# Tile stage of a six-layer attention kernel: four pieces issued at other places

## What is computed

```python
for i in range(DEPTH):                       # 6 layers
    x = attn_layer(shift_tokens(x), ...) + x
    x = ffn_layer(shift_tokens(x), ...) + x
# attn_layer: q, k, v = x @ Wqkv   (16 heads of 64)
#   q = l2norm(q) * qs; k = l2norm(k) * ksc; rotate both by tables (cos, sin, scale)
#   windows of 32 tokens see their own and the previous window:
#   sim = q k^T * 8, masked; attn = softmax(sim); out = attn v; out @ Wo
# ffn_layer: xn = layernorm(x); a, gate = split(xn @ W1 + b1)
#   a * gelu(gate) @ W2 + b2
```

## Time and profile before

| | us |
|---|---|
| runs | 2463.4 (median), 2463.25, 2467.93 |
| profiled execution | 2469.18 |
| its span (first to last instruction) | 2467.4 |
| busy in the span: PE | 2082.4 (84%) |
| DVE | 1832.7 (74%) |
| ACT | 1507.3 (61%) |
| POOL | 1163.3 (47%) |

### The profile page before, as it was taken

The page is one execution under the profiler, slowest core; times in us unless marked ns, Lnnn a source line. Parts: engine busy times, 40 slices in busy tenths (PEclk is TensorE's granted clock), DMA queues, the critical chain, the costliest instruction groups (busy, mean ns, idle before and its releaser), DMA issues.

```text
span 2467.4 us, 87755 instructions
## 1 busy us (share of the span) xinstructions
PE 2082.4 (84%) x34492; PEld 1484.1 (60%) x34492; DVE 1832.7 (74%) x3797; ACT 1507.3 (61%) x2993; POOL 1163.3 (47%) x1373
## 2 busy tenths in 40 slices
PE   6888899876688888888888898888888888888886
PEld 4556654454466666666566665666666666666663
DVE  6777855576687787777777877787687777777873
ACT  4666733364566676666766666666666666766663
POOL 1111100001666666555665556666566655665660
PEclk9999999997899999999999999999999999999998
DMA  4000000001121232222222212222222222222221
GB/s 101 2 2 1 2 1 0 1 1 43 51 69 52 51 87 70 60 65 56 78 62 69 59 52 78 68 71 52 63 77 66 62 67 63 77 60 58 64 57 30
DMA packets 94732, 126.36 MB, mean 51 GB/s; under 512 B 27485, under 2 KB 42467, under 8 KB 94307
## 3 DMA queue, kind: packets, MB, share of 16 engines
q1 hardware_dynamic: 94306, 120.54, 18.7%
HBM read 21.91 MB, written 1.05 MB: 9 GB/s over the span
## 4 chain that ended last, share of the span: by engine, by line
PE 43%; DVE 17%; issue 11%; ACT 9%; POOL 1%; ACTq 0%; DVEq 0%; DMA 0%; POOLq 0%; SPq 0%
PE pj L567 10%; PE sc L567 10%; PE oo L567 10%; PE tr L570 8%; ACT arena L1782 7%; PE tr L567 5%; DVE arena L1608 3%; DVE arena L1614 3%; DVE arena L1606 2%; DVE xn L1225 1%; DVE arena L1628 1%; DVE arena L1630 1%; PE oo L570 1%; DVE stats L1212 1%; ACT sc L1782 0%
## 5 line engine op out<-in xcount | busy, mean ns | idle before, releaser
L2172 POOL TENSOR_TENSOR arena<-arena 128x1024 f32<-128x1024 f32 x192 | 456.7, 2379 | 260.2 <-DVE arena L1608 249.1
L1782 ACT ACTIVATE arena<-tr 128x512 f32<-128x512 f32 (+2 forms) x874 | 456.5, 571 | 136.2 <-PE tr L570 86.4
L1782 ACT ACTIVATE arena<-pj 128x512 f32<-128x512 f32 x576 | 333.9, 592 | 264.0 <-PE pj L567 259.7
L570 PE MATMUL tr<-ident,arena 128*128 128x128 f32 x2974 | 435.2, 282 | 67.1 <-ACT arena L1782 53.3
L1782 ACT ACTIVATE arena<-arena 128x16 f32<-128x16 f32 (+6 forms) x808 | 354.9, 453 | 212.3 <-DVE arena L1623 113.6
L1606 DVE TENSOR_TENSOR arena<-pj,rtab 128x512 f32<-128x512 f32 x384 | 262.9, 685 | 275.2 <-ACT arena L1782 174.9
L570 PEld LDWEIGHTS tr<-ident,arena 128*128 128x128 f32 x2974 | 345.6, 143 | 152.8 <-issue 59.1
L2188 POOL TENSOR_TENSOR arena<-arena 128x1024 f32<-128x1024 f32 x192 | 370.4, 1929 | 17.9 <-POOL arena L2184 1.2
L567 PE MATMUL oo<-slab,arena 64*32 64x64 f32 (+1 forms) x12416 | 234.0, 230 | 59.4 <-issue 24.7
L1608 DVE TENSOR_TENSOR arena<-pj,rtab 128x512 f32<-128x512 f32 x384 | 261.5, 681 | 0.0
L1614 DVE TENSOR_REDUCE arena<-arena 128x8 f32<-128x512 f32 x384 | 259.6, 676 | 0.0
(11 more groups left out here) (275 smaller groups left out, 3824.3 us busy)
## 6 DMA issues: line engine op xcount, KB each, us to landing
slab<-arena SPq DMA_DIRECT2D x576, 128.0 KB
slab<-arena SPq DMA_DIRECT2D x336, 64.0 KB
wqkv<-in_L_ffn_Wqkv SPq DMA_DIRECT2D x18, 512.0 KB, 3.5
wo<-in_L_ffn_Wo SPq DMA_DIRECT2D x6, 512.0 KB, 4.2
w<-in_L_ffn_W SPq DMA_DIRECT2D x6, 341.0 KB
YT<-in_L_attn_x SPq DMA_DIRECT2D x4, 256.0 KB, 3.7
arena<-in_L_ffn_W SPq DMA_DIRECT2D x1, 1024.0 KB
out_x<-arena SPq DMA_DIRECT2D x4, 256.0 KB, 2.2
```

The lines of the kernel that those rows point to most:

```text
L570: return nc.tensor.transpose(o, i, ident[0:i.shape[0], 0:i.shape[0]])
L1782: return nc.scalar.activation(o, i, f, **k)
L2172: p_.tensor_tensor(r_, r_, rb[:, k, :], ALU.add).then_inc(sum_ok, 1)
```

## The change

Four pieces are issued at other places in `slot`. No operation is added or taken away.

1. PE, t = 0: `ff_up(m2, 2)` now stands before `window_scores(g - 1, .., 1)` instead of behind it.
2. DVE: `tables(l + 1)` stands at the start of b = 2, t = 0 instead of the end of b = 1, t = 2.
3. ACT: the exponential of tile g-1 is no longer the last step of slot g; it stands in slot g+1 (there as tile g-2) between `square(g, 0)` and `square(g, 1)`.
4. ACT, t = 3: the output copies `out_` stand before `ln_finish` instead of behind it.

The order of steps inside each moved piece is kept, and its semaphores count one tile further back, since it now runs one slot later.

```diff
@@ PE
                 if t != 0 and d_:
                     out_()
-                if c_:
-                    window_scores(g - 1, (t - 1) % T, 1)
                 if t == 0 and m2 is not None:
                     pe.wait_ge(on_ok, g - 1 if d_ else NTILE)
                     ff_up(m2, 2)
+                if c_:
+                    window_scores(g - 1, (t - 1) % T, 1)
                 if t == 0 and d_:
                     out_()
@@ DVE
+                if new and b == 2 and t == 0:
+                    tables(l + 1)
                 if new:
...
-                if new and b == 1 and t == 2:
-                    tables(l + 1)
@@ ACT
                 def exp_():
-                    ac.wait_ge(t_sub, g)
-                    wait(ac, e_tr, g * 2 - 2)
-                    wait(ac, sm_ok, g - 1)
+                    ac.wait_ge(t_sub, g - 1)
+                    wait(ac, e_tr, g * 2 - 4)
+                    wait(ac, sm_ok, g - 2)
...
                 if new:
                     wait(ac, ss_ok, g * 4 - 1)
                     square(g, 0)
+                if d_:
+                    exp_()
+                if new:
                     wait(ac, ss_ok, g * 4)
                     square(g, 1)
...
+                if d_:
+                    out_()
                 if t == 3 and m1 is not None:
                     ac.wait_ge(lc_ok, m1 + 1)
                     ln_finish(LNB, LNB_BANKS[1], m1, lcur[:, 0:1], lcur[:, 1:2], hB)
-                if d_:
-                    out_()
                 if new:
                     inverse_root(g, 1)
                     copy_v(g, t, 1)
-                if c_:
-                    exp_()
```

## The result

| | before | after |
|---|---|---|
| median of the runs, us | 2465.66 (four runs) | 2376.65 (four runs) |
| fastest and slowest, us | 2463.25, 2469.19 | 2372.35, 2377.54 |
| profiled execution, us | 2469.18 | 2377.54 |
| its span, us | 2467.4 | 2375.7 |
| granted clock over the whole | 0.974 | 0.976 |

The ratio of the times is 0.9634, with a 95% interval of 0.9616 to 0.9653: the changed kernel is faster by 89.0 us in the medians and by 91.7 us in the span of the two profiled executions. The prediction was 2390.8 us with a range of 2374 to 2424, from a gain of 72.6 us. Direction, mechanism and range held; the gain was some 16 us larger than forecast, and so lies outside the 60 to 77 us that had the largest chance (0.40), in the class of rival (a) and a little more (0.24).

What follows compares the result with a forecast made beforehand. PE was taken to set the pace, losing time in short waits mostly ended by ACT. Terms of 42.7 + 4.5 - 1.2 + 27.6 + 7 = 80.6 us, less 8 for late instructions, gave 72.6: median 2390.8 us, range 2374 to 2424.

Steps and rivals of the forecast that it cites:

- rival (a): Nothing is lost to late PE instructions: 80.6 us less, median 2382.8; chance 0.24, with gains up to 95 us.
- What bounds the kernel: PE sets the pace and loses time in short waits; ACT ends the longest, 134.8 us between 700 and 2400 us.
- The up-product and the exponential: t = 0 to t = 1: PE's waits shrink by 2.1 us per sequence, 1.4 at b = 3; 42.7 us.
- The exponential at the other slots: Gains 4.5 us from t = 2 to t = 3, loses 1.2 at t = 0 of b = 0, otherwise 0.
- The norm's end: t = 3: PE's wait for the output copies before the output product goes, except part at b = 3; 27.6 us.
- The tables: Moved to b = 2, they hide in DVE's idle time and shorten PE's norm wait at b = 1; 7 us.
- What may eat of it: PE instructions that arrive late take back 8 us, a quarter of 33 us of waits without a releaser.
- The gross of 80.6: Sum of the forecast's terms in us before the deduction for late instructions: 42.7 + 4.5 - 1.2 + 27.6 + 7.
- (b): PE's transposes release DVE at t = 1, so the first term is 1.2 per sequence: gain 53 us, median 2410; chance 0.11.
- (c): Late PE instructions take half of the gross: gain 40 us, median 2423; chance 0.11.
- (d): No change: ACT and DVE give back what each piece gains, as when later soft1 holds ACT; chance 0.04.
- (e): Slower: ACT held longer at the exponential, PE waits 2.8 us at t = 1, clock drops; +19 us, median 2482; chance 0.06.

Runs made afterwards that it cites:

- the first experiment: The changed kernel with the exponential put back at the end of its slot, the other three pieces still moved: 2400.4 us, ratio 0.9724.
- norm first: The changed kernel with DVE's `ln_apply` at t = 3 put before the sums of the squares: 2372.5 us, ratio 0.9603.
- copy first: The changed kernel with ACT's last value copy of t = 0 put before its inverse root: 2379.2 us, ratio 0.9628.

## Why the prediction was right, and where it was off

**What bounds the kernel: right.** PE set the pace, ACT's ends of a few chains set PE's waits, and taking those waits away gave the time: the four rows fell by 68.8 us and the time by 89. A removed wait gave some 0.16 us more than its listed length (below), and pauses without a releaser went with them.

**The up-product and the exponential: mechanism right, size a little low.** The signs it named came out as follows: 0.77 instead of 0.5 before the second projection; 1.89 instead of 2.4 us of DVE idling before soft1; no wait before the down-product. Predicted were 2.1 us per plain sequence, 1.2 from the up-product and 0.9 from the exponential. The table of starts shows 0.39 + 0.95 + 0.94 = 2.28 in the sequence that the prediction had read, but 1.9 in a plain one, 0.95 and 0.94. Two readings were off. The half of the scores was priced at 1.2 us from 1669.55 to 1670.73, a stretch that holds the pause of 0.16; where no pause stands, the third up-product starts 1.11 us behind the last value projection before and 0.23 now, so the chain on ACT begins 0.88 us earlier and not 1.2. And b = 3 gained the same 1.9 as the others, where 1.4 was forecast. Over the 22 sequences it is 3.8 + 21.0 + 20.6 = 45.4 us against 42.7, and 3.8 of the 45.4 are pauses that went. The runs give 52 to 54 us for the two parts against 46.0 with the other slots; most of what is above lies in the pause of the draining pipeline and in the filling (below). The order of the two pieces itself cost and saved nothing, as predicted. Whether the pauses went because the instructions stand at other positions or for another reason, no run here tells apart.

**The exponential at the other slots: the size about right, by another path.** At t = 3 of the sequence that was traced, the probabilities' transposes come 0.61 us earlier, counted from the down-product. PE's wait for ACT before them fell from 1.50 to 1.01 us; it stood in the trace and the prediction didn't name it, though it is part of the 44.2 us of the earlier trace rows. But the norm then has PE wait 0.44 us longer (0.58 to 1.02). The prediction let the norm's wait shrink by 0.25; it grew, since PE got there sooner than DVE. Over the stage it is 18.0 to 20.5 us, +2.5, where -4.5 was forecast. From the down-product to the output product the exponential's move is worth 3.7 us over the 22 sequences when it is undone and 2.3 when it is done alone, against 4.5 - 1.2 = 3.3; two executions of the changed kernel differ by 2.7 us there, so this is no proof.

**The norm's end: right** (27.6 forecast, 28 measured by undoing it), by two errors that cancel. At b = 3 waits of 5.3 us in sum stayed, up to 1.47, instead of 5 times 0.67, since the split of the next key weights and its load stand in front, which I had named and not priced. In the other sequences a removed wait gave more than its listed length: 1.46 for 1.30, 1.75 for 1.58.

**The tables: not told.** 7 forecast, 3 to 4 by the runs, 3 to 8 by the starts, and by the runs alone not told from nothing. The mechanism is seen: b = 1 is 1.8 to 2.0 us a pass shorter. At b = 2 the tables do stand in an idle stretch: they end at 1604.73, and DVE still waits 0.35 us for ACT's square before it rotates (1605.08).

**What may eat of it: wrong, by the whole 8 us.** The step that failed took the pauses named "issue" to grow when waits ahead of them go. Their sum fell, 47.9 to 40.0, and another of 2.40 us, behind 2400 us, went too. Rival (a) was right. A reading was off as well: the four edges make 2.68 + 2.65 + 2.82 + 2.40 = 10.6 us of the sum, not about 15, so 37 us were left for the other places and not 33. The Trainium skill (Runtime: NRT & Kernel Launch, Instruction fetch mechanics) holds that fetching in straight code is hidden and that only a taken branch breaks it. Its result for the sum was right. Its reason isn't what the traces show: pauses of 0.88 and 0.95 us stand in straight code, and these two moved by 16 products when 16 were put in front.

**How the sum closes.** The gross of 80.6 was made of 5.5 passes, 14.7 a pass. The four middle passes gained 14.7 each. Of the 91.7 us of the span, 11 lie beyond 80.6, and most of them lie where the pipeline fills and drains, which the prediction didn't count: 3.1 us before the first output product, 3.1 after the last one, and 3.8 instead of 1.8 in the second sequence, which has no feed-forward part behind it. In the filling, ACT's exponential stood on the way of every tile; there PE's waits before transposes, some of the first in the stage, fell from 2.22 and 1.92 us to 1.73 and 1.42. The runs bear this out: the first output product starts at 681.8 to 682.2 us in the three traces with the exponential in its old place and at 677.3 to 679.8 in the eleven with it moved. In the draining it is the up-product and the pause of 2.40 us.

So for the medians: 80.6, less no supply, plus some 8 from the two ends, is 89. That it closes so well is partly luck, as the terms above are off in both directions by 3 to 8 us.

**The rivals.** (b) falls by the first experiment. (c) and (d) fall by the time. For (e), slower through a low clock, the largest wait of PE for ACT outside the edge is now 1.5 us. The granted clock was 0.50 (1.2 instead of 2.4 GHz) for at least 4 us behind three of the four edges of the changed kernel. The windows (us; busy us of PE, PE's weight load, DVE, ACT, POOL; granted clock; DMA share; GB/s) behind the third edge and around the first:

```profile
1732.00:1736.00 4.00, 3.47 (x71) 2.51 (x72) 3.82 (x10) 0.00 (x0) 0.92 (x1) 0.50 0.59 168
1150.00:1166.00 16.00, 9.47 (x170) 6.62 (x168) 11.74 (x28) 8.09 (x16) 7.75 (x12) 1.00 0.42 112
```

The prediction let one wait of about 2.7 us decide. These rows don't bear that out. The waits at the four edges were 2.54, 2.61, 2.48 and 2.82 us; behind the first the clock stayed at 1.00, and behind the others it fell only 5 to 6 us later, where the kernel before had it low right behind its 2.82.

## What to carry to other kernels

When one engine sets the pace and loses its time in short waits, list the waits by what ended them, find the few places in the code where they stand, and move what stands ahead of the late step on the *other* engine, first of all work whose reader is far off. Price it from start to start, not by the listed waits, and count the stretches where a pipeline fills and drains by themselves. A second move of the same sort is to be tried against the next end in the queue: here two of the three later ones, norm first and copy first, shortened the wait they aimed at and gave it back at the next one.

## What the runs showed of the hardware that I had not expected

**DVE and POOL hold each other up.** The tables' operations in their new place show it. The durations of line 1669 in the changed kernel (least, median and greatest, ns), then DVE and POOL there:

```profile
L1669 DVE TENSOR_TENSOR wT<-rot,qks x28: 277/283/1997, 617.4 to 2178.1; 128x128 f32<-128x128 f32 x28
```

```profile
1602.41 1.96 POOL L2189 TENSOR_TENSOR arena<-arena 128x1024 f32<-128x1024 f32 x1
...
1602.54 2.19 DVE L1669 TENSOR_TENSOR wT<-rot,qks 128x128 f32<-128x128 f32 x2
```

An operation of 0.28 us takes up to 2.00 when it begins behind the start of a product on POOL; before, the greatest of the 28 was 0.30. It happened to one pair in each of the six layers, and line 1669 is 10.1 us busier in sum. It cost nothing, since DVE would have waited for ACT's square anyway. It works in the other direction too, and there DVE gained: its split of the key weights, line 1657, took 16.6 us in sum before and 10.0 after. These two changes are the only ones above 0.5 us among the operations listed for DVE, and they leave some 5 of its 8.5 us of busy time without a name. At the loop's edge of the kernel before, POOL began first (1803.07) and DVE's split of the key weights took 3.41 us; in the changed kernel DVE began first and took 1.22, and it was POOL that was late, with 3.23 us instead of 2.36:

```profile
1803.07 2.36 POOL L2172 TENSOR_TENSOR arena<-arena 128x1024 f32<-128x1024 f32 x1 [0.24 <-POOL xs_lo L2200]
...
1803.10 3.41 DVE L1657 TENSOR_TENSOR w_lo<-wqkv,wk_hi 128x1024 fp32r<-128x1024 f32 x1
```

```profile
1745.19 1.22 DVE L1657 TENSOR_TENSOR w_lo<-wqkv,wk_hi 128x1024 fp32r<-128x1024 f32 x1
...
1745.39 3.23 POOL L2173 TENSOR_TENSOR arena<-arena 128x1024 f32<-128x1024 f32 x1 [0.24 <-POOL xs_lo L2201]
```

This is what the Trainium skill (SBUF — State Buffer, Who interferes with whom) says of a DVE instruction with two inputs from SBUF beside a GpSimd instruction that reads SBUF: it contends, since its second input comes through the shared read interface. The traces agree in both directions.

**PE's pauses sit at fixed places of its stream.** Most moved with the code by as many products as were put in front, and lasted 0.2 to 1.8 us; those at the loop's edge went from 2.5 to 2.8 us to 3.7 to 3.9 us when the code ahead grew by 16 products. Start to start a pause cost 0.2 to 0.3 us more than it is listed with.
